# One product set for keys and queries of four heads, placed by ten DMAs, in a fused vision-transformer kernel

## The chip, the cores and the metric

The program runs on one core of a Trainium2 chip. The time is the device time of one execution in microseconds (us). Engines: PE (TensorE, matrix products), DVE (VectorE), ACT (ScalarE), POOL (GpSimd), SP (SyncE, which here only issues DMAs). Each engine runs its own instructions in program order and waits on semaphores that the others raise. "Hop" below is the time between the end of one operation and the start of the one on another engine that it releases.

## What is computed

For each of 128 images (3 x 224 x 224) the kernel computes a patch embedding (196 tokens of 192 numbers, a layer norm before and after), a causal attention with 12 heads of 16 dimensions and a relative term, and a routed block (sigmoid score per token; the 29 tokens of the lowest scores get attention over all tokens, the others a gated mixture; then an MLP 192-768-192 with gelu). Cut to what the change touches:

```python
h = tok(x)                                   # patches, LN, @W + b, LN
qkv = LN(h) @ w_attn + b_attn                # q, k, v; 12 heads of 16
q = q * 16 ** -0.5
scores = q @ k.T + q @ rel.T                 # so the keys are k + rel
probs = softmax(where(causal, scores, -inf))
h = h + (probs @ v) @ w_proj + b_proj
h = h + routed_block_and_mlp(LN(h))
```

## The kernel before

All weights stay in SBUF. Products that need near-float32 accuracy are made in a reduced format (F32R) from parts: a number is a high part plus a low part, and a product takes `PAIRS`, five matmuls over the two chunks of the 192 input columns. T is 196 tokens, HT 98, NG 3 groups of four heads.

**Four images are in work at once.** A pass of the loop (`step(k, m, n, l, ...)`, L313) does the last stage (`tail`: the MLP's `up`, gelu, `down`, `output`) for image k, the middle (`back`: the routed block) for k + 1, the causal attention (`front`) for k + 2 and the embedding (`head`) for k + 3. Each engine has the calls of a pass written out by hand in one fixed order; that order is the schedule. The steady loop makes 124 passes; passes before and after fill and drain it. PE's list also has 36 matmuls for keys and queries in each pass.

**Keys and queries before.** At the start of a pass PE's `keys` and `queries` (both through `group_cols`, L698 to L712) make for each of the three groups a [128, 196] product: five matmuls with `wk` or `wq` (L705) and one for bias and relative term (L711, L708). Of the 128 output rows, a head has 32: its 16 dimensions twice ("doubled columns"), the first 16 for the high part, the second 16 for the low part. ACT copies (L1589, L1584), DVE makes the low part (L1230, L1224). The keys go to `kparts`, and SP's `place_keys` (L428) puts them with four DMAs of 32 partitions into `kz`, where head s has its own columns and the other heads' rows are zero; queries stay in `qparts`. A score unit (`causal("S0")` to `"S8"`, L740 and L743) multiplies `qparts` by four heads of `kz`.

**Around it on PE**, in the order of a pass: `routed_cols` (transposes of `z`, L679), `score` and `keys2` (L695, `nTs`), `mlp_cols` (L679), `values` (L687, `wv`), `values2`, `mixing_rows` (L687), S0 to S2, `gather`, S3, `weighted_sum`, `qsel` (L857), S4, `embed(0)` (L754), S5 to S7, `scores2` (L865 to L867, needs DVE's `q_blocks`), S8, `square_sums`, transposes A0 to B2 (L778) between `embed(1)`, `up(0)`, `transposes2`, `up(1)` and `context2`, then `attention` (L929, L936: the sum over values, called y), `attn_out` (L907), `up(2)`, `projection` (L948), `scatter`, `attention_cols` (L679, `a_row`), `down` (L982).

**Around it on DVE and POOL.** DVE: `routed_cols_lo` (L1209, L1211), `q_blocks` (L1356, L1359), `max2` (L1365, L1368), `embedding` (L1274 with its statistics L1187 and L1190), `h1_stats` (L1187, `bn_a`), `attention_input` (L1195, `a_row`). POOL: nine `normalised` units (L539), `rstd` (L512, L514), the softmax division of the routed block (L584, "pn2" below), the two operations that make `h1` (L596, L598), `gelu_low` (L530).

Of the kernel before, what the change touches and what calls it, by code (L numbers as in the profile page):

```python
# [38 lines left out]
T = GR * GR  # L39
# [29 lines left out]
    x_in=len(XROWS) * 16, out_done=16, kz_in=4 * 16,  # L69

    tok_mm=1, sqs_mm=1, zT_mm=1, score_mm=1, mrow_mm=1, usum_mm=1, kk_mm=1, vv_mm=1, aT_mm=1, q_mm=1, k_mm=1, v_mm=1,
# [4 lines left out]
    tok_var=1, tok_y=1, y_stat=1, y_norm=1, h1_stat=1, a_sb=1, aTs_sb=1, klo_sb=1,  # L76
    qparts_sb=1, rowmax=9, rden_sb=9, pT_dve=len(PT) - len(PT_ACT), h2_sb=1,
# [3 lines left out]
    sq_sb=1, aT_sb=1, qhi_sb=1, khi_sb=1, v_sb=1, probs=9, pT_act=len(PT_ACT), yhi_sb=2,  # L81
# [14 lines left out]
def build(nc, ins, out):  # L96
    W = dict(ins)
    with ExitStack() as ctx:
# [32 lines left out]
        widths = dict(wq=NG * 128, wk=NG * 128, wv=D, fwk=D, fwv=D, fwm=D, wr=HT, w1=F)  # L131
        split = {name: sb(name + "_split", [128, 4, width], F32R)
                 for name, width in widths.items()}
        bk = sb("bk", [128, NG])
# [3 lines left out]
        relk = sb("relk", [128, NG, T], F32R)  # L138
        add_parts = sb("add_parts", [128, 128], F32R)
        onesr = sb("onesr", [128, T], F32R)  # L140
        bqparts = sb("bqparts", [128, NG * 128], F32R)
# [42 lines left out]
        qk_parts = sb("qk_parts", [128, 2, NG, T], F32R)  # L184
        qhi, qparts = (qk_parts[:, i] for i in range(2))

        table_out = sb("table_out", [1, 1])
        kz = sb("kz", [128, 2, 4, NG, T], F32R)
# [10 lines left out]
        yhi, yparts = qhi, qparts  # L199
# [55 lines left out]
        kparts = gparts[:, :, 0:NG]  # L255
# [7 lines left out]
        relb = flat[:, 2 * F:2 * F + NG * T].rearrange("p (g t) -> p g t", g=NG)  # L263
# [6 lines left out]
        bqrow = p0[:].rearrange("p h t -> p (h t)")[:, 0:NG * 128]  # L270
# [3 lines left out]
        for i, name in enumerate(("wq", "wk")):  # L274
            size = 2 * widths[name]
            raw[name] = flat[:, i * size:(i + 1) * size].rearrange("p (c w) -> p c w", c=2)
# [109 lines left out]
        for s in range(4):  # L386
            for r in (0, DH):
                at = 32 * s + r
                load(bk[at:at + DH], ba[1, s])
                load(wp[at:at + DH], wpr[s])  # L390
# [1391 lines left out]
```

## Time and profile before

| | |
|---|---|
| median of 3 runs | 5028.85 us (5027.4 to 5029.55) |
| the profiled execution, its own time | 5031.06 us |
| its span, first to last instruction | 5029.3 us |
| PE busy | 4843.7 us, 96% |
| DVE, ACT, POOL busy | 79%, 70%, 64% |
| DMA engines, mean busy | 43.3% |
| granted TensorE clock, mean | 0.988 |

A PE that counts as busy is one with a matmul in flight; since matmuls overlap, the length of a stretch is read from the start of one group to the start of the next, not from the groups' own lengths. The loop repeats exactly: the attention product of one pass starts at 2500.43 us, that of the next at 2538.41, 37.98 us later. A row of the timeline gives start, length, engine, line, operation, operands, count, and in brackets the idle time ahead of it with what ended it.

### The profile page before, as it was taken

The numbers are of one execution on the slowest core, as the hardware profiler recorded it, in microseconds if no ns is written. First come the engines' busy times: TensorE is split into PE (matmuls) and PEld (weight loads), VectorE is DVE, ScalarE is ACT, GpSimd is POOL, SyncE is SP. The second block draws the span as 40 slices with busy tenths as digits, with TensorE's granted clock in tenths as the row PEclk, the third lists the DMA queues.
The fourth block names the chain that finished last, engine by engine and source line by source line (L and its number), as shares of the span: only waits on it lengthen the run. The fifth ranks groups of instructions, "written<-read, shape, count | busy, mean of one in ns | idle before, by whom it ended". The sixth has DMA issues, their size and how long they took to land. (4 is left out here: it accounts for less than half of the span.)

```text
span 5029.3 us, 146877 instructions
## 1 busy us (share of the span) xinstructions
PE 4843.7 (96%) x46680; PEld 4523.8 (90%) x46680; DVE 3993.2 (79%) x12888; ACT 3540.8 (70%) x12158; POOL 3230.6 (64%) x4399
## 2 busy tenths in 40 slices
PE   3999999999999999999999999999999999999998
PEld 2899999999999999999999999999999999999997
DVE  3788888888888888888888888888888888888885
ACT  0677777776777777777777677777777777777775
POOL 2566666666666666666666666666666666666664
PEclk6999999999999999999999999999999999999999
DMA  5444444444444445444444444444444444444440
GB/s 68 56 65 62 55 64 61 59 62 61 61 59 64 61 55 67 62 55 65 61 59 62 61 61 59 64 61 56 67 62 55 65 61 59 62 61 61 59 64 16
DMA packets 338231, 302.00 MB, mean 60 GB/s; under 512 B 46796, under 2 KB 305177, under 8 KB 338201
## 3 DMA queue, kind: packets, MB, share of 16 engines
q1 hardware_dynamic: 325950, 298.98, 43.3%
q10 hardware_dynamic: 12251, 2.65, 0.4%
q8 instruction: 15, 0.25, 0.0%
q14 instruction: 15, 0.12, 0.0%
HBM read 205.18 MB, written 19.27 MB: 45 GB/s over the span
## 5 line engine op out<-in xcount | busy, mean ns | idle before, releaser
L1615 ACT ACTIVATE p<-banks,negmax 98x98 f32<-98x98 f32 (+1 forms) x3072 | 1138.9, 379 | 184.8 <-DVE negmax L1237 121.3
L539 POOL TENSOR_TENSOR p<-p,rden 98x392 f32<-98x392 f32 x1152 | 953.6, 842 | 384.0 <-DVE rden L1253 379.5
L1237 DVE TENSOR_REDUCE negmax<-banks 98x2 f32<-98x392 f32 (+1 forms) x1152 | 626.2, 553 | 51.4 <-PE banks L743 51.2
L743 PE MATMUL banks<-kz,qk_parts 128*98 128x392 f32 x2304 | 632.8, 385 | 0.0
L778 PE MATMUL banks<-ident,p 98*98 98x98 f32 x4608 | 550.7, 251 | 69.9 <-ACTq L1619 64.4
L1615 ACT ACTIVATION_READ_ACCUMULATOR p<-banks,negmax 98x1 f32 x3072 | 610.3, 199 | 0.0
L754 PE MATMUL banks<-tokw,x_sb 128*98 128x193 f32 x3072 | 572.7, 336 | 15.5 <-POOLq L551 15.5
L530 POOL TENSOR_TENSOR gparts<-gT,gparts 128x392 fp32r<-128x392 f32 x384 | 398.3, 1050 | 270.8 <-DVE gparts L1433 270.8
L754 PEld LDWEIGHTS banks<-tokw,x_sb 128*98 128x98 f32 x3072 | 541.7, 252 | 18.0 <-issue 15.5
L778 PEld LDWEIGHTS banks<-ident,p 98*98 98x98 f32 x4608 | 415.8, 129 | 140.0 <-ACTq L1619 90.8
L695 PE MATMUL banks<-z3Ts,w_split 128*128 128x196 f32 x3840 | 534.7, 286 | 4.8 <-DVE z3Ts L1211 3.9
L695 PEld LDWEIGHTS banks<-z3Ts,w_split 128*128 128x128 f32 x3840 | 477.9, 194 | 9.1 <-DVE z3Ts L1211 4.9
L982 PE MATMUL banks<-w,gparts 128*98 128x192 f32 x4608 | 441.2, 254 | 2.6 <-issue 2.6
L554 POOL TENSOR_TENSOR gstore<-gstore 128x588 f32<-128x588 f32 x128 | 155.2, 1213 | 447.0 <-ACT gstore L1600 447.0
L1690 ACT ACTIVATE gT<-banks,bf 128x196 f32<-128x196 f32 x768 | 285.5, 426 | 206.6 <-PE banks L695 206.6
L1680 ACT ACTIVATE f<-h,shift,rstdf 98x192 f32<-98x192 f32 x256 | 126.5, 541 | 426.3 <-DVE shift L1449 426.3
L982 PEld LDWEIGHTS banks<-w,gparts 128*98 128x98 f32 x4608 | 422.5, 164 | 2.9 <-issue 2.9
L514 POOL TENSOR_TENSOR rstd<-ve,nhalf 98x2 f32<-98x2 f32 x512 | 360.5, 704 | 72.7
L1623 ACT COPY pT<-banks 98x392 f32<-98x392 f32 x768 | 358.7, 480 | 68.1 <-PE banks L778 50.2
L743 PEld LDWEIGHTS banks<-kz,qk_parts 128*98 128x98 f32 x2304 | 322.1, 166 | 40.3
L740 PE MATMUL banks<-tri,identh 98*98 98x196 bf16 (+1 forms) x1152 | 323.3, 281 | 5.4 <-DMA kz<-gparts 3.8
L1593 ACT ACT_TABLE_LOAD x252 | 323.3, 1283 | 4.5
(273 smaller groups left out, 12470.1 us busy)
## 6 DMA issues: line engine op xcount, KB each, us to landing
x_sb<-in_x SPq DMA_DIRECT2D x384, 196.0 KB, 5.0
kz<-gparts SPq DMA_DIRECT2D x512, 147.0 KB, 2.9
x_sb<-in_x SPq DMA_DIRECT2D x256, 190.8 KB, 8.8
x_sb<-in_x SPq DMA_DIRECT2D x256, 185.5 KB, 10.9
x_sb<-in_x SPq DMA_DIRECT2D x128, 189.0 KB, 7.3
out<-out_row SPq DMA_DIRECT2D x128, 147.0 KB
pT<-in_L_ffn_W ACTq DMA_DIRECT2D x1, 576.0 KB
gstore<-in_L_ffn_W SPq DMA_DIRECT2D x1, 384.0 KB
```

What stands on the lines that cost most here:

```text
L514: gp.tensor_tensor(r, ve, nhalf[:], ALU.pow).then_inc(sem[name], 1)
L530: gp.tensor_tensor(gparts[:, 1, at], gT[:, j % 2], gparts[:, 0, at].bitcast(F32), ALU.subtract).then_inc(sem["gparts_sb"], 1)
L539: gp.tensor_tensor(heads, heads, rden[:, g, t, s0:s0 + sn].unsqueeze(2).broadcast_to([HT, sn, w]), ALU.mult).then_inc(sem["pnorm_sb"], 1)
L695: last = mm(o, w[:, wpart, lo:hi], src[:, p], start=i == 0, stop=i == len(PAIRS) - 1)
L740: mm(masked, identh[:], tri[:].unsqueeze(1).broadcast_to([HT, len(slots), HT]), start=True, stop=False, skip_group_check=True)
L743: last = mm(o, qparts[:, g, HT * t:HT * t + HT], kz[:, part, slots[0]:slots[-1] + 1, g, 0:w], start=False, stop=part == 1, skip_group_chec ...
L754: last = mm(bank[b][0:HT, t * (D + 1):(t + 1) * (D + 1)], xf[:, a:a + (HT - 1) * PS + 1:PS], tokw[:, q], start=t == 0 and q == 0, stop=q = ...
L778: last = pe.transpose(bank[b][0:HT, HT * i:HT * i + HT], src, ident[0:HT, 0:HT])
L982: last = mm(bank[7][0:HT, t * D:(t + 1) * D], gparts[:, part, f, HT * t:HT * t + HT], w2[:, wpart, f], start=f == 0 and t == 0 and i == 0, ...
L1237: ve.tensor_reduce(negmax[:, g, t, slots[0]:slots[-1] + 1], bank[RING[f"S{k}"]][0:HT, 0:w * len(slots)].rearrange("p (s w) -> p s w", w=w) ...
L1615: sc.activation((p1 if t else p0)[0:HT, 4 * g + s], bank[b][0:HT, w * i:w * i + w], ACT.Exp, bias=negmax[:, g, t, s:s + 1], accum_out=den[ ...
L1623: sc.copy(pt_dst(name[0], int(name[1:])), bank[RING[name]][0:HT, 0:4 * HT]).then_inc(sem["pT_act"], 1)
```

## The change

Keys and queries of four heads (a group) come out of one product set: the weight `wkq` has for each group 64 columns of keys and 64 of queries, without doubling, so that 18 matmuls a pass take the place of 36. Bias and relative term come in one matmul per group (`add_w`, `rel_ones`). ACT makes the high part of all 128 rows (`kq[:, 0]`), DVE the low part (`kq[:, 1]`). High and low parts of the scores' operands then have to be on different partitions, and that is now done by DMAs: eight of 16 partitions put the keys of a head twice into `kz`, two of 64 partitions put the queries into `qparts` (high part to partitions 0 to 63, low to 64 to 127). They start when the low part is there (`kqlo_sb`), and S0 waits for them (`kz_in`, `q_in`).

The product set is moved from the start of the pass that uses it to the end of the pass before, between `scatter` and `down`; `attention_cols` moves ahead of `up(2)` and writes bank 2 (was 1); the attention product y goes to banks 0 and 1 (was 2 and 3). `yhi` and `yparts` are tiles of their own. SP issues the placement after the next image's prefetch. The order of many other calls changes on all engines: `embed(0)` ahead of `values2`, `embed(1)` after S4, `qsel` after it, `up(0)` and `up(1)` together before S8, `transposes2` and `context2` earlier, `attn_out` before B2.

```diff
@@ SP @@
-                sp.wait_ge(sem["klo_sb"], after("klo_sb", n))
+                sp.wait_ge(sem["kqlo_sb"], after("kqlo_sb", n))
                 for s in range(4):
-                    at = slice(32 * s, 32 * s + 32)
-                    sp.dma_start(kz[at, :, s].bitcast(F32),
-                                 kparts[at].bitcast(F32)).then_inc(sem["kz_in"], 16)
+                    for r in range(2):
+                        at = 64 * r + DH * s
+                        sp.dma_start(kz[at:at + DH, s].bitcast(F32),
+                                     kq[DH * s:DH * s + DH].bitcast(F32)).then_inc(
+                                         sem["kz_in"], 16)
+                for part in range(2):
+                    sp.dma_start(qparts[64 * part:64 * part + 64].bitcast(F32),
+                                 kq[64:128, part].bitcast(F32)).then_inc(sem["q_in"], 16)
...
             with sp.Fori(0, B - 4) as j:
-                place_keys(j + 2)
                 prefetch(j + 3, j + 4)
+                place_keys(j + 3)
                 store(j)
@@ PE @@
-                def queries():
-                    if back:
-                        pe.wait_ge(sem["h2_sb"], all_before("h2_sb", n))
-                    pe.wait_ge(sem["aTs_sb"], after("aTs_sb", n))
-                    group_cols(0, split["wq"], "q_mm")
+                    pe.wait_ge(sem["aTs_sb"], after("aTs_sb", l))
+                    for g in range(NG):
+                        o, at = grouped(2)[:, g], slice(128 * g, 128 * g + 128)
+                        for i, (p, wpart) in enumerate(PAIRS):
+                            mm(o, split["wkq"][:, wpart, at], aT[:, p], start=i == 0, stop=False)
+                        last = mm(o, add_w[:, at], rel_ones[:], start=False, stop=True)
+                    last.then_inc(sem["kq_mm"], 1)
...
                         if k == 0:
-                            pe.wait_ge(sem["qparts_sb"], after("qparts_sb", n))
+                            if back:
+                                pe.wait_ge(sem["h2_sb"], all_before("h2_sb", n))
+                            pe.wait_ge(sem["q_in"], after("q_in", n))
                             pe.wait_ge(sem["kz_in"], after("kz_in", n))
...
-                    out_of = [bank[2 + g // 2][:, (g % 2) * T:(g % 2) * T + T] for g in range(NG)]
+                    out_of = [bank[g // 2][:, (g % 2) * T:(g % 2) * T + T] for g in range(NG)]
@@ DVE @@
                 def keys():
 
-                    ve.wait_ge(sem["khi_sb"], after("khi_sb", n))
-                    ve.tensor_tensor(kparts[:, 1], grouped(2), kparts[:, 0].bitcast(F32),
-                                     ALU.subtract).then_inc(sem["klo_sb"], 1)
+                    ve.wait_ge(sem["kqhi_sb"], after("kqhi_sb", l))
+                    ve.tensor_tensor(kq[:, 1], grouped(2), kq[:, 0].bitcast(F32),
+                                     ALU.subtract).then_inc(sem["kqlo_sb"], 1)
@@ the loads of the weights, once @@
-                for j, name in enumerate(("wq", "wk")):
-                    for r in (0, DH):
-                        load(raw[name][p:p + size, chunk].rearrange(
-                                 "p (h e) -> p h e", e=32)[:, :, r:r + DH],
-                             wa[lo:hi, j * D:(j + 1) * D].rearrange("p (h e) -> p h e", e=DH))
+                for j, at in enumerate((D, 0)):
+                    load(halves(raw["wkq"][p:p + size, chunk])[:, j],
+                         wa[lo:hi, at:at + D].rearrange("p (g w) -> p g w", g=NG))
```

**PE, from the attention product into the next pass.** Before (the two branch rows are the turn of the loop; the group of five and one stands three times for each product set):

```order
L948 MATMUL banks<-wps,qk_parts 98x192 x12
L915 MATMUL banks<-ao,selT 98x192 x4
L679 MATMUL banks<-ident,a_row 128x98 x2
L679 MATMUL banks<-ident,a_row 64x98 x2
L982 MATMUL banks<-w,gparts 98x192 x36
L313 UNCONDITIONAL_BRANCH
L313 ISA
L705 MATMUL banks<-aT,wk_split 128x196 x5
L711 MATMUL banks<-relk,add_parts 128x196
```

After:

```order
L699 MATMUL banks<-z3Ts,w_split 128x196 x10
L943 MATMUL banks<-wps,yparts 98x192 x12
L910 MATMUL banks<-ao,selT 98x192 x4
L718 MATMUL banks<-aT,wkq_split 128x196 x5
L719 MATMUL banks<-rel_ones,add_w 128x196
...
L977 MATMUL banks<-w,gparts 98x192 x36
L313 UNCONDITIONAL_BRANCH
L313 ISA
L683 MATMUL banks<-ident,z 128x98 x2
```

The product set now stands ahead of `down` (L982, now L977), and a pass begins with the transposes of `z`; the queries' set, which stood between those transposes and `score`, is gone.

**DVE, from `q_blocks` to the statistics of the embedding.** Before (`max2` is the two reductions to 128 partitions; rows of `z3Ts`, `pT`, `mean`, `var` and others follow it, and L1274 of `embedding` comes thirteen rows on):

```order
L1365 TENSOR_REDUCE negmax<-banks 128x2
L1368 TENSOR_REDUCE negmax<-banks 128x1
L1208 REGISTER_ALU
L1209 TENSOR_TENSOR z3Ts<-banks,z3Ts 128x196
L1211 TENSOR_TENSOR z3Ts<-banks,z3Ts 64x196
L1253 RECIPROCAL rden<-den 98x4
L1245 COPY pT<-banks 98x392
```

After:

```order
L1345 TENSOR_TENSOR qb<-qs,slot_of 128x256
L1348 TENSOR_TENSOR qb<-qs,slot_of 64x128
L1224 REGISTER_ALU
L1226 TENSOR_REDUCE negmax<-banks 98x2
L1224 REGISTER_ALU
L1226 TENSOR_REDUCE negmax<-banks 98x4
L1242 RECIPROCAL rden<-den 98x2
L1354 TENSOR_REDUCE negmax<-banks 128x2
L1357 TENSOR_REDUCE negmax<-banks 128x1
L1242 RECIPROCAL rden<-den 98x2
L1263 SCALAR_TENSOR_TENSOR y_row<-banks,rstd,tok_bias 98x192 x2
L1182 BN_STATS bn_y<-y_row 98x6 x2
```

`embedding` stands right behind `max2`, so it cannot start before `scores2` has been made.

**POOL, from the embedding's second `rstd` to `h1`.** Before:

```order
L584 TENSOR_TENSOR probs_<-probs_,rden 128x588
L537 REGISTER_ALU
L539 TENSOR_TENSOR p<-p,rden 98x392
L512 TENSOR_TENSOR ve<-mv_y,epsc 98x2
```

After:

```order
L516 TENSOR_TENSOR ve<-mv_y,epsc 98x2
L518 TENSOR_TENSOR rstd<-ve,nhalf 98x2
L586 TENSOR_TENSOR probs_<-probs_,rden 128x588
L541 REGISTER_ALU
L543 TENSOR_TENSOR p<-p,rden 98x392
```

Pn2 stood ahead of that `rstd` and stands behind it now, with three `normalised` units after it (two of which stood ahead of it before) and then the two operations for `h1`.

## Rows read from the trace of the kernel before

**Rows 1.** Timeline of PE: start us, length us, line, operands, count, [idle ahead].

```profile
2505.58 3.43 PE L982 MATMUL banks<-w,gparts 128*98 128x192 f32 x36
2508.84 0.73 PE L705 MATMUL banks<-aT,wk_split 128*128 128x196 f32 x5
...
2510.86 0.50 PE L679 MATMUL banks<-ident,z 98*128 98x98 f32 x4
2511.14 0.78 PE L705 MATMUL banks<-aT,wq_split 128*128 128x196 f32 x5
...
2515.10 1.11 PE L687 MATMUL banks<-wv_split,aT 128*98 128x192 f32 x10
2517.85 0.33 PE L740 MATMUL banks<-tri,identh 98*98 98x392 bf16 x1
...
2525.04 0.25 PE L740 MATMUL banks<-tri,identh 98*98 98x196 bf16 x1
...
2526.45 0.49 PE L865 MATMUL banks<-kk,qb 128*128 128x196 f32 x2
...
2527.45 0.25 PE L740 MATMUL banks<-tri,identh 98*98 98x196 bf16 x1
...
2528.54 2.26 PE L754 MATMUL banks<-tokw,x_sb 128*98 128x193 f32 x12
2530.50 1.40 PE L695 MATMUL banks<-z3Ts,w_split 128*128 128x196 f32 x10
...
2533.06 0.88 PE L778 MATMUL banks<-ident,p 98*98 98x98 f32 x8 [0.48 <-ACTq L1619]
...
2540.62 1.39 PE L695 MATMUL banks<-z3Ts,w_split 128*128 128x196 f32 x10
```

**Rows 2.** Timeline of ACT, same pass.

```profile
2511.60 0.33 ACT L1572 CAST nTs<-banks 128x196 fp32r<-128x196 f32 x1
...
2522.64 0.46 ACT L1561 ACTIVATE qs<-banks,fbqs 128x32 f32<-128x32 f32 x2 [0.68 <-PE banks L857]
```

**Rows 3.** Timeline of DVE, same pass.

```profile
2511.74 0.77 DVE L1230 TENSOR_TENSOR gparts<-banks,gparts 128x588 fp32r<-128x588 f32 x1 [0.42 <-ACT gparts L1589]
...
2512.79 0.36 DVE L1211 TENSOR_TENSOR nTs<-banks,nTs 64x196 fp32r<-64x196 f32 x1
...
2519.07 0.65 DVE L1321 TENSOR_SCALAR ez<-ez 98x2 f32<-98x2 f32 x1
...
2523.47 0.28 DVE L1359 TENSOR_TENSOR qb<-qs,slot_of 64x128 f32<-64x128 f32 x1
...
2527.79 0.55 DVE L1365 TENSOR_REDUCE negmax<-banks 128x2 f32<-128x392 f32 x1
...
2532.64 0.74 DVE L1274 SCALAR_TENSOR_TENSOR y_row<-banks,rstd,tok_bias 98x192 f32<-98x192 f32 x2 [0.54 <-POOL rstd L514]
...
2539.60 0.60 DVE L1187 BATCH_NORM_STATS2 bn_a<-h 98x6 f32<-98x192 f32 x2
...
2541.97 0.65 DVE L1195 TENSOR_SCALAR a_row<-h,mv_a,rstd 98x192 f32<-98x192 f32 x2
```

**Rows 4.** Timeline of POOL, same pass.

```profile
2518.98 0.72 POOL L558 TENSOR_TENSOR sqsum<-gstore 128x196 f32<-128x196 f32 x1
...
2532.56 1.17 POOL L584 TENSOR_TENSOR probs_<-probs_,rden 128x588 f32<-128x588 f32 x1
...
2535.49 0.84 POOL L539 TENSOR_TENSOR p<-p,rden 98x392 f32<-98x392 f32 x1
...
2537.96 1.01 POOL L598 TENSOR_TENSOR h<-y_row,ln2b 98x384 f32<-98x384 f32 x1
```

**Rows 5.** Timeline of SP's DMA queue, same pass.

```profile
2512.54 2.52 SPq L431 DMA_DIRECT2D kz<-gparts  x4
```

**Rows 6.** The page, section 6: DMA issues, KB each, median us from issue to landing.

```profile
kz<-gparts SPq DMA_DIRECT2D x512, 147.0 KB, 2.9
```

**Rows 7.** Timeline of DVE at the start of the program.

```profile
55.51 0.46 DVE L1091 COPY pT<-bv 128x294 f32<-128x294 f32 x1 [30.33 <-DMA pT<-in_L_ffn_W]
```

More of the change, by code:

```diff
@@ L565, in step @@
                     normalised(1)
-                if back:
-                    gp.drain()
-                    gp.tensor_tensor(h2b[:], h2[:], both(bf2), ALU.add).then_inc(sem["h2b_sb"], 1)
+                if head:
+                    gp.wait_ge(sem["tok_var"], after("tok_var", l))
+                    rstd(var1[:], ve1[:], rstd1[:], "tok_rstd")
                 if front:
@@ L576, in step @@
                     normalised(5)
[L577 to L578 removed]
                 if head:
[L580 to L581 removed]
+                    gp.wait_ge(sem["y_stat"], after("y_stat", l))
+                    rstd(mv_y[:, :, 1], ve2[:], rstd2[:], "y_rstd")
                 if back:
@@ L587, in step @@
                 if front:
+                    normalised(6)
+                if front:
                     normalised(7)
-                if head:
-                    gp.wait_ge(sem["y_stat"], after("y_stat", l))
-                    rstd(mv_y[:, :, 1], ve2[:], rstd2[:], "y_rstd")
                 if front:
@@ L603, in step @@
                     rstd(mv_a[:, :, 1], ve3[:], rstd3[:], "h1_rstd")
+                if tail:
+                    gelu_low(0)
+                if back:
+                    gp.drain()
+                    gp.tensor_tensor(h2b[:], h2[:], both(bf2), ALU.add).then_inc(sem["h2b_sb"], 1)
                 if tail:
@@ L990, in attention_cols @@
                     pe.wait_ge(sem["a_sb"], after("a_sb", l))
-                    rows_to_cols(1, a_row, "aT_mm")
-                if front:
-                    keys()
+                    if front:
+                        pe.wait_ge(sem["pT_act"], after("pT_act", n, evacuation("B1")[1]))
+                    rows_to_cols(2, a_row, "aT_mm")
                 if back:
@@ L997, in step @@
                 if front:
-                    queries()
+                    values()
+                if tail:
+                    mlp_cols()
                 if back:
@@ L1001, in step @@
                     keys2()
-                if tail:
-                    mlp_cols()
-                if front:
-                    values()
+                if head:
+                    embed(0,0,QX)
                 if back:
@@ L1022, in step @@
                 if head:
-                    embed(0,0,QX)
+                    embed(1,0,3)
+                    embed(1,3,QX)
+                if back:
+                    qsel()
                 if front:
@@ L1059, in step @@
                     attention()
-                if back:
-                    attn_out()
+                if head:
+                    attention_cols()
                 if tail:
@@ L1068, in step @@
                 if head:
-                    attention_cols()
+                    keys()
                 if tail:
@@ L1698, in step @@
                 if front:
+                    values()
                     load_table(ACT.Exp)
-                    queries()
                 if back:
+                    exp_scores()
                     keys2()
+                if tail:
+                    mlp_cols_hi()
                 if head:
```

249 lines of the change are left out of this document (107 added, 142 removed).

## The prediction

> **What bounds the kernel now.** I read the busy shares first, then the period of the loop, then one pass of the timeline on each engine. PE is busy 96% of the span, DVE, POOL and ACT less (the table under the profile's heading), so PE's list of matmuls sets the time. The loop repeats at 37.98 us, and 37.98 x 124 is 4710 of 5029 us; what the change does to one pass counts about 125 times. PE's timeline of a pass marks a single wait of size, 0.48 us ahead of the transposes at 2533.06, for ACT's softmax; everything else starts where the group before it lets go [rows 1]. I put another 0.5 us into gaps too short for the timeline to mark, by a count of columns against the distances between groups: an estimate. So waits hold PE for about 1.0 us of a pass, and removed matmuls are worth their full length only as long as nothing that PE waits for becomes the later one. That is the question of this change: PE gets shorter, and the chains through ACT, DVE, POOL and now SP get no shorter.
>
> **Removed matmuls.** The keys' set of 18 holds PE from 2508.84 to 2510.86, 2.02 us, 0.112 us a matmul [rows 1]. Half of 36 go: -2.02 us a pass. The remaining 18 have the same shapes.
>
> **Placement and S0.** Before, `keys` ends at 2510.86 and SP's first placement goes out at 2512.54 [rows 5]: 1.68 us for ACT's copy and DVE's low part, which itself takes 0.77 [rows 3]. Four issues take 2.52 us, 0.63 each, and one lands 2.9 us after its issue [rows 5, 6]. After, ten go out: nine spacings of 0.63 are 5.67, and the last lands 2.9 later, 8.57. From the end of the product set to S0's data: 1.68 + 8.57 = 10.25 us. PE's work in that time: the stretch from `down` to S0, 2505.58 to 2517.85, is 12.27 us and holds both product sets, 2 x 2.02; `embed(0)` comes into it, as long as its twin `embed(1)`, 2528.54 to 2530.50, 1.96 [rows 1]. So 12.27 - 4.04 + 1.96 = 10.19, and with a wait of 0.3 for `score` (below) 10.5. The placement is hidden by 0.25 us, hence at nothing, with all of that work as its cover; each 0.1 us that it is later costs 12.5 us in all. Eight of the ten carry half the bytes (16 partitions), and if spacing follows bytes the sum falls to 1.68 + 8 x 0.32 + 0.63 + 2.9 = 7.8: slack 2.7. If instead an issue waits for engines that work on few partitions, it grows; the lower end is no cost, the upper one is the second rival. I take no cost, since the nearest row counts issues and I gave it no credit for size. SP's prefetch now stands ahead of the placement and its store behind; the prefetch waits for buffers that are free long before, which I cost at nothing.
>
> The Trainium skill speaks against the shape of these DMAs. Its page "SBUF — State Buffer", section "Door 1: The DMA port swizzle", has it that bandwidth follows how many of 16 ports the partitions reach, with 104 GB/s on 16 partitions and 189 on 32. By that price alone a DMA of 16 partitions would take 0.7 us of transfer, about what one of 32 with twice the bytes takes, eight and two in a row some 7.3 us, and the last would land at 11 us after the product set instead of 10.25. The rows of before hold only DMAs of 32 partitions, so no row here decides it.
>
> **Three legs whose cover shrinks.** On each, PE waits for other engines' answer to its own product.
>
> (a) *From `scores2` to `attention_cols`.* `embedding` now stands behind `max2` on DVE, pn2 and three `normalised` units stand between the embedding's second `rstd` and h1 on POOL. The chain: from the end of `scores2` (the group behind it starts at 2527.45 [rows 1]) to DVE's start at 2527.79 is 0.34, then 0.55 and about 0.3 for the second, smaller reduction, and a reciprocal, 0.1: 1.3 [rows 3]. From `embedding`'s L1274 at 2532.64 to POOL's unit behind `rstd` at 2535.49: 2.85. Pn2: 1.17. Three units at 0.84, packed a little closer: 2.4. The two operations of h1, 1.01 each with a drain between: 2.15 [rows 3, 4]. From `bn_a` at 2539.60 to the end of `a_row` at 2542.62: 3.02, of which 0.4 goes, because `gelu_low` no longer stands ahead of that `rstd`; a hop, 0.1. Sum: 1.3 + 2.85 + 1.17 + 2.4 + 2.15 + 2.62 + 0.1 = 12.6 us. PE's work from the end of `scores2` to `attention_cols`: 2527.45 to 2540.62 is 13.17, less `embed(1)` 1.96, the wait 0.48, square sums 0.3 and the short gaps 0.3, plus S7, 0.45: 10.6 [rows 1]. So PE waits 2.0 us in this leg whatever it does; the first of it, about 0.9, at `transposes2`, which needs pn2 (1.3 + 2.85 + 1.17 = 5.3 us behind `scores2`, where PE has 4.4 us to do), then at `attn_out` and `attention_cols`. With hops counted twice here and there I take 1.9; the ends are 1.4 and 2.3.
>
> (b) *From `qsel` to `scores2`.* ACT's `qs` starts at 2522.64, DVE's `qb` ends at 2523.47 + 0.28: 1.11 us, with two hops 1.35 [rows 2, 3]. Before, PE had S4, `embed(0)` and S5 to S7 to do there. Now it has S5 and S6: three such units take 2525.04 to 2526.45, two 0.95 [rows 1]. PE waits 0.4 (0.2 to 0.6).
>
> (c) *From the transposes of `z` to `score`.* Before, the queries' set, 2 us, covered ACT's and DVE's copies into `nTs`: ACT starts at 2511.60, DVE ends at 2512.79 + 0.36, 1.55 us [rows 2, 3], of which up to 0.4 is `kparts`' low part (0.77) in the way, now gone. The cover is now `values`, about 1.0, and `mlp_cols`, the same four transposes as 2510.86 to 2511.14, 0.28 [rows 1]. With a hop: a wait of 0.3 (0 to 0.45).
>
> New waits: 1.9 + 0.4 + 0.3 = 2.6 us. The old ones, 1.0, go, since their causes lie inside the longer ones: a PE that has waited finds the softmax behind it done. The pass: -2.02 + 2.6 - 1.0 = **-0.4 us**, 37.98 to 37.6; over 125 passes -50 us. With the ends of the terms: -1.2 to +0.2 us a pass.
>
> **One-time parts.** At the start DVE waits 30.33 us for the last weight load [rows 7]; fourteen loads fewer, and runs of 64 bytes made into runs of 256, let that end earlier. I take -10 (-18 to -4). Filling the pipeline costs a placement of ten with nothing to hide it, +4 to +5. On ACT and DVE the new parts are as many copies of 588 columns less one pair; neither engine is the bound. The banks of y and its own tiles take a reuse wait away and cost nothing: DVE has `a_row` (0.65 [rows 3]) done as the last of leg (a), not behind y.
>
> **Sum.** -50 - 10 + 5 = -55. The profiled execution took 5031.06, 2.2 above the median of 5028.85; against the median: 4974, say **4975 us**.
>
> **Rivals.** *The full gain.* If the chains are shorter than I add them up (units run beside one another closer, or the new order leaves no queue), PE's saving shows: -2.02 x 125 = -253, with the one-time parts 4770; with half of the new waits (-2.02 + 1.3 - 1.0) x 125 = -215, 4810; with three quarters 4890. For it: PE at 96%. Against it: the order of DVE and POOL, which puts leg (a) in a row. Chance 0.15.
>
> *The placement ends last, slower.* S0 waits for `kz_in` and `q_in`. The point is 0.25 us of lateness behind 10.25. If a DMA of 16 partitions holds its queue for as long as one of 32 and lands as late as the second half of them (each issue 0.72 instead of 0.63, landing 3.3), S0's data come at 1.68 + 6.5 + 3.3 = 11.5, 1.0 us late; a part of it takes the place of the wait in leg (c) and of leg (a)'s, which starts over behind S6 and does not shrink, so 0.5 to 0.8 us a pass stay: 4975 + 62 to 100 = 5037 to 5075. At 0.2 us it is 5000. For it: DVE's and PE's work is all ahead of it in one line. Against it: half the bytes. Chance 0.17, 0.12 of it slower.
>
> *`q_blocks` is held by POOL.* DVE's `ez`, two numbers a partition, takes 0.65 us and ends at 2519.72; POOL's operation beside it ends at 2519.70 [rows 3, 4]. DVE operations on SBUF do wait here for POOL's. `q_blocks` reads two SBUF tiles and now stands, by my sum, 0.2 us clear of a `normalised` unit of 0.84. If it falls behind it, leg (b) and everything behind `scores2` are later by up to 0.84, about 0.7: +88, **5060 us**. Chance 0.08. The Trainium skill, page "SBUF — State Buffer", section "SBUF: two separate sides", calls this pair of ports an exclusive lock, held for the whole instruction, also for a DVE operation with two SBUF inputs against a POOL one that reads SBUF; the `ez` rows agree, and by that rule such an operation waits as computed.
>
> *It does nothing that shows*: the set is halved and another order of the same waits gives the period back, 5020 to 5038. Chance 0.05.
>
> **How the numbers follow.** Forecast 0.55 (its own range 4950 to 5000), full or half gain 0.15, placement 0.17, held `q_blocks` 0.08, nothing 0.05. A measurement of this kernel tells 0.2%, 10 us, from no change. Faster by more: 0.55 + 0.15 + 0.02 = 0.72; within it 0.03 + 0.05 = 0.08; slower 0.12 + 0.08 = 0.20. The range leaves out the fuller gains (0.08) and the later placements and a held `q_blocks` (0.12): 4905 to 5050.
>
> **What the profile after would show.** Right: a period of 37.6 us; 18 matmuls in 2.0 us behind `scatter`; marked PE waits at `transposes2` (0.9, for POOL's pn2), `attn_out` (0.5), `scores2` (0.4, for DVE's `qb`) and `score` (0.3); S0 without a wait; ten placements at 0.63 or closer, landing 2.9; the idle time at the start shorter by some 10. Wrong: S0 idle ahead of it for a DMA (the placement); `qb`'s L1359 longer than 0.28, or late (the lock); marked waits under 2 us a pass (the full gain), or over 3.5, which would say that a chain I added up has another link.

## The result and the profile after

The changed kernel takes 4967.28 us, the median of 4 runs (4967.15 to 4967.44), against 5029.01 (4 runs, 5027.4 to 5029.55): a ratio of 0.9878, 95% interval 0.9861 to 0.9895. That is 61.7 us less, where 54 were forecast. Its profiled execution has a span of 4965.4 us, 63.9 less than the one of before.

The page of the changed kernel, section 1, columns as in the table of before, and section 6:

```profile
PE 4645.9 (94%) x44376; PEld 4282.1 (86%) x44376; DVE 3884.0 (78%) x12759; ACT 3468.4 (70%) x12030; POOL 3263.1 (66%) x4399
...
kz<-kq SPq DMA_DIRECT2D x1024, 73.5 KB, 2.6
...
qparts<-kq SPq DMA_DIRECT2D x256, 147.0 KB, 2.7
```

PE is busy for 197.8 us less and the span is 63.9 us shorter, so PE's idle time grew by 134 us. The waits of PE that the profile marks, in the whole execution (us in total, times, longest):

```profile
PE banks L869 <- POOL probs_ L586: 93.2, 127, 2.7
PE banks L902 <- DVE ctxT L1378: 37.7, 127, 1.4
PE banks L683 <- DVE a_row L1190: 37.5, 125, 10.5
...
PE banks L699 <- DVE y_row L1263: 23.6, 125, 0.2
PE banks L699 <- DVE nTs L1206: 19.2, 118, 0.7
```

The kernel before had one such row of size that comes back in every pass:

```profile
PE banks L778 <- ACTq L1619: 64.4, 130, 1.5
```

One pass of PE's timeline, changed kernel, what answers to [rows 1]:

```profile
2506.76 0.87 PE L902 MATMUL banks<-fwo,ctxT 128*66 128x192 f32 x4 [0.28 <-DVE ctxT L1378]
...
2509.82 0.55 PE L683 MATMUL banks<-ident,a_row 98*128 98x98 f32 x4 [0.21 <-DVE a_row L1190]
...
2512.77 0.73 PE L718 MATMUL banks<-aT,wkq_split 128*128 128x196 f32 x5
...
2514.78 3.38 PE L977 MATMUL banks<-w,gparts 128*98 128x192 f32 x36
...
2519.24 0.50 PE L683 MATMUL banks<-ident,z 98*128 98x98 f32 x4
2519.89 0.70 PE L699 MATMUL banks<-nTs,wr_split 128*98 128x196 f32 x5 [0.16 <-DVE nTs L1206]
...
2525.34 0.33 PE L733 MATMUL banks<-tri,identh 98*98 98x392 bf16 x1
...
2533.03 0.33 PE L733 MATMUL banks<-tri,identh 98*98 98x392 bf16 x1
...
2533.81 0.60 PE L860 MATMUL banks<-kk,qb 128*128 128x196 f32 x2
...
2536.80 1.33 PE L699 MATMUL banks<-z3Ts,w_split 128*128 128x196 f32 x10 [0.18 <-DVE y_row L1263]
2537.98 0.25 PE L733 MATMUL banks<-tri,identh 98*98 98x196 bf16 x1
...
2538.42 0.84 PE L771 MATMUL banks<-ident,p 98*98 98x98 f32 x8
2539.98 0.86 PE L869 MATMUL banks<-ident,probs_ 128*98 128x128 f32 x6 [0.72 <-POOL probs_ L586]
...
2542.81 1.22 PE L771 MATMUL banks<-ident,p 98*98 98x98 f32 x12
2544.32 0.87 PE L902 MATMUL banks<-fwo,ctxT 128*66 128x192 f32 x4 [0.29 <-DVE ctxT L1378]
```

`attn_out` (L902) starts at 2506.76 and at 2544.32. A single pass differs from the next by some hundredths of a microsecond, so the period is better read over many: between the fourth and the 126th `attn_out` are 122 passes, from 291.51 to 4872.24 us here (37.55 each) and from 297.85 to 4934.69 before (38.01). 0.46 x 124 = 57 us is the loop's part of the 63.9. The periods of the experiments below are read over one or two passes. The product set lies between 2512.77 and 2514.78, 2.01 us for 18 matmuls. S0 (2525.34) has no wait marked. Between S6 (2533.03) and `scores2` (2533.81) are 0.78 us; a unit of four heads has 0.54 elsewhere in the pass (S3, 2527.74 to 2528.28), so 0.25 is a wait for `qb` that isn't marked.

**What a mark leaves out.** A mark counts idle time from the end of the last matmul as the profile draws it, and that end lies behind the point where the next one could have started. The eight transposes at 2538.42 have a row of 0.84 us; in `v_diag2` below, where nothing is waited for behind them, the next group starts 0.69 after the first of them (2526.45 to 2527.14). Here it starts 1.56 after (2538.42 to 2539.98): a delay of 0.87 where the mark says 0.72. A delay below some 0.15 (0.84 less 0.69) can stay without a mark. So delays are read below from start to start, against the same group where nothing holds it. The same reading of the kernel before:

```profile
2531.74 0.84 PE L778 MATMUL banks<-ident,p 98*98 98x98 f32 x8
...
2535.95 1.04 PE L778 MATMUL banks<-ident,p 98*98 98x98 f32 x8
2536.92 1.09 PE L884 MATMUL banks<-scratch,vv 98*64 98x128 f32 x12
```

From 2531.74 to 2533.06 [rows 1] are 1.32 us for eight transposes, a delay of 0.6 where the mark says 0.48, and from 2535.95 to 2536.92 are 0.97, a delay of 0.25 without a mark. S3 takes 0.73 (2520.26 to 2520.99) where a unit of four heads has 0.54, another 0.2.

POOL and SP, same pass of the changed kernel:

```profile
2533.20 0.41 POOL L516 TENSOR_TENSOR ve<-var,epsc 98x2 f32<-98x2 f32 x1 [1.99 <-DVE var L1256]
...
2534.42 3.24 POOL L543 TENSOR_TENSOR p<-p,rden 98x392 f32<-98x392 f32 x4
...
2538.76 1.17 POOL L586 TENSOR_TENSOR probs_<-probs_,rden 128x588 f32<-128x588 f32 x1
2539.88 2.47 POOL L543 TENSOR_TENSOR p<-p,rden 98x392 f32<-98x392 f32 x3
...
2543.45 1.00 POOL L599 TENSOR_TENSOR h<-y_row,ln2b 98x384 f32<-98x384 f32 x1
```

```profile
2516.46 5.00 SPq L429 DMA_DIRECT2D kz<-kq  x8
2521.50 1.24 SPq L433 DMA_DIRECT2D qparts<-kq  x2
```

From 2533.20 to 2544.45 POOL works almost without a gap: leg (a) runs through its queue. SP issues ten placements in 6.28 us, 0.62 to 0.63 apart, those of 16 partitions as those of 64.

At the start of the program, DVE's wait for the last weights, and SP's first loads of `w_attn`, in the changed kernel and (second fence) in the kernel before:

```profile
46.50 0.46 DVE L1085 COPY pT<-bv 128x294 f32<-128x294 f32 x1 [20.48 <-DMA pT<-in_L_ffn_W]
...
14.34 3.34 SPq L411 DMA_DIRECT2D p<-in_L_attn_w_attn  x2
```

```profile
14.19 10.45 SPq L414 DMA_DIRECT2D p<-in_L_attn_w_attn  x3
```

Such a row merges issues. The three of before, each read in a window of its own (the second starts at 14.77, the third at 21.76): 0.54 and 6.95 us for two loads of 128 rows in runs of 64 bytes, then 2.88 for the values' weights, which have runs of 768. The two of after: 0.58 for one in runs of 256, 2.72 for the values' weights.

The wait is 9.9 us shorter than in [rows 7]; at the first `a_row` the changed kernel is 10.6 us ahead (98.48 against 109.07 us).

### The profile page after: what moved, and what is told of

Its sections match the earlier page's. It is cut to its first block and busy times, and to the rows that moved or that the text cites. A ratio compares the mean times of both kernels' runs of the same rounds, so it can differ in the third digit from the quotient of the medians.

```text
span 4965.4 us, 143019 instructions
## 1 busy us (share of the span) xinstructions
PE 4645.9 (94%) x44376; PEld 4282.1 (86%) x44376; DVE 3884.0 (78%) x12759; ACT 3468.4 (70%) x12030; POOL 3263.1 (66%) x4399
## 5 line engine op out<-in xcount | busy, mean ns | idle before, releaser
L736 PE MATMUL banks<-kz,qparts 128*98 128x392 f32 x2304 | 650.7, 386 | 0.0
L1226 DVE TENSOR_REDUCE negmax<-banks 98x2 f32<-98x392 f32 (+1 forms) x1152 | 614.9, 550 | 40.6 <-PE banks L736 40.5
L699 PE MATMUL banks<-z3Ts,w_split 128*128 128x196 f32 x3840 | 508.3, 280 | 25.8 <-DVE y_row L1263 23.6
L771 PE MATMUL banks<-ident,p 98*98 98x98 f32 x4608 | 481.6, 250 | 3.6 <-ACTq L1600 3.6
L977 PE MATMUL banks<-w,gparts 128*98 128x192 f32 x4608 | 434.3, 252 | 0.5 <-POOL gparts L534 0.4
L977 PEld LDWEIGHTS banks<-w,gparts 128*98 128x98 f32 x4608 | 422.9, 163 | 0.8 <-POOL gparts L534 0.8
L1604 ACT COPY pT<-banks 98x392 f32<-98x392 f32 x768 | 343.7, 478 | 40.7 <-PE banks L771 28.4
L736 PEld LDWEIGHTS banks<-kz,qparts 128*98 128x98 f32 x2304 | 321.8, 166 | 28.6
L1570 ACT CAST kq<-banks 128x588 fp32r<-128x588 f32 x128 | 83.2, 650 | 350.7 <-PE banks L719 350.7
## 6 DMA issues: line engine op xcount, KB each, us to landing
kz<-kq SPq DMA_DIRECT2D x1024, 73.5 KB, 2.6
```

Source lines behind the costliest of these rows:

```text
L699: last = mm(o, w[:, wpart, lo:hi], src[:, p], start=i == 0, stop=i == len(PAIRS) - 1)
L736: last = mm(o, qparts[:, g, HT * t:HT * t + HT], kz[:, slots[0]:slots[-1] + 1, part, g, 0:w], start=False, stop=part == 1, skip_group_chec ...
L771: last = pe.transpose(bank[b][0:HT, HT * i:HT * i + HT], src, ident[0:HT, 0:HT])
L977: last = mm(bank[7][0:HT, t * D:(t + 1) * D], gparts[:, part, f, HT * t:HT * t + HT], w2[:, wpart, f], start=f == 0 and t == 0 and i == 0, ...
L1226: ve.tensor_reduce(negmax[:, g, t, slots[0]:slots[-1] + 1], bank[RING[f"S{k}"]][0:HT, 0:w * len(slots)].rearrange("p (s w) -> p s w", w=w) ...
L1604: sc.copy(pt_dst(name[0], int(name[1:])), bank[RING[name]][0:HT, 0:4 * HT]).then_inc(sem["pT_act"], 1)
```

## The experiments

**The matmuls alone.** The kernel before with three matmuls for each group instead of six; nothing else is touched.

```diff
-                    for i, (p, wpart) in enumerate(PAIRS):
+                    for i, (p, wpart) in enumerate(PAIRS[:2]):
```

> The kernel before, its order unchanged, with three matmuls instead of six in each of the six groups for keys and queries: 18 matmuls a pass are gone (the other products of the parts are left out, so keys and queries are coarse), and nothing is placed, moved or reordered. If PE's list alone sets the time: 2.02 us a pass less, 5029 - 253 = 4776 us. If the legs through the other engines take it back: the queries' set (now 1.07 us) covers less of the copies into nTs, so that PE waits some 1.0 to 1.4 us at score, and only 0.6 to 0.9 us a pass are left: 4917 to 4955 us.

Measured: 4969.22 us, ratio 0.9872 (0.9856 to 0.9889), some 60 us less than before. The period is 37.53 us (two passes of `attn_out`, 2469.98 to 2545.03), the same as the changed kernel's. PE's waits name the place (the old wait for ACT's softmax stays, 64.2 us in all):

```profile
PE banks L695 <- DVE nTs L1211: 179.5, 127, 2.1
```

1.41 us a pass are marked at `score`. From start to start, 1.69 us lie between the queries' last matmul and `score`, in the mean of the loop's passes, where the kernel before has 0.18: 1.51 of delay have come. -2.02 + 1.51 = -0.51, and the period fell by 0.48 (38.01 to 37.53): this account closes. The legs theory holds, PE's list alone does not, though even the legs theory was 14 us too hopeful. It is also the best measure of the new order: with 18 matmuls less, the old order got as much while it waited in one new place as the new one gets while it waits in six. (It couldn't have them without the new placement, since there the parts of 64 columns lie elsewhere.)

**The order with the old matmuls.** The changed kernel, product set made twice in its place.

```diff
-                        for i, (p, wpart) in enumerate(PAIRS):
-                            mm(o, split["wkq"][:, wpart, at], aT[:, p], start=i == 0, stop=False)
-                        last = mm(o, add_w[:, at], rel_ones[:], start=False, stop=True)
+                        for again_ in range(2):
+                            for i, (p, wpart) in enumerate(PAIRS):
+                                mm(o, split["wkq"][:, wpart, at], aT[:, p], start=i == 0, stop=False)
+                            last = mm(o, add_w[:, at], rel_ones[:], start=False, stop=True)
```

> The changed kernel with its product set of 18 matmuls made twice, in the place where it stands: the new order, placement and banks with as many matmuls as before. If the removed matmuls are worth their full 2.02 us at that place and the rest of the gain was lost by the new order's waits: 2.0 us a pass more, 4969 + 254 = 5223 us, some 190 us above the kernel before. If the new order were no worse than the old one with the same matmuls: 5029 us.

Measured: 5222.14 us, ratio 1.0387 (1.0369 to 1.0404). The period is 39.59 us (2474.69 to 2553.86 in two passes), 2.05 more than the changed kernel's. At this place, between `scatter` and `down`, outside every leg, a matmul costs and saves its full length, and all waits of the changed kernel stay as they were. So the change of -0.46 is -2.05 for the matmuls and +1.6 for waits that order and shorter cover bring, less the old ones that went.

**Ten matmuls outside and inside leg (a).** Both double a product of ten matmuls in the changed kernel.

```diff
@@ values2 @@
-                    cols_to_rows(5, nTs, split["fwv"], "vv_mm")
+                    for part in range(2):
+                        for t in range(2):
+                            for i, (p, wpart) in enumerate(PAIRS):
+                                last = mm(bank[5][0:HT, t * D:(t + 1) * D],
...
@@ up @@
-                    for f in (2 * j, 2 * j + 1):
+                    for f in (2, 3, 2, 3) if j == 1 else (2 * j, 2 * j + 1):
```

> The changed kernel with values2 made twice: ten more matmuls of 192 columns, 0.9 to 1.0 us, between embed(0) and S0, outside the leg from scores2 to attention_cols. Both theories expect the full price, 0.9 to 1.0 us a pass: 5080 to 5093 us. A result much below that would say that S0 was waiting for something that the trace does not mark.

> The changed kernel with up(1) made twice: ten more matmuls of 196 columns, 1.2 us, between scores2 and transposes2. If PE's list sets the time: 1.2 us a pass, 5117 us. If POOL and DVE set the time of the leg from scores2 to attention_cols, the waits at transposes2 (0.72), attn_out (0.28) and attention_cols (0.21) take it up, all but what S8's softmax and its copies come later: 0.3 to 0.8 us a pass, 5005 to 5067 us, with the wait for pn2 at transposes2 gone.

Measured: `values2` twice 5079.67 us, ratio 1.0094 (1.0077 to 1.0111), a period of 38.46 (2481.66 to 2558.57 in two), +0.92: the full price. `up(1)` twice 5042.66 us, ratio 1.0021 (1.0012 to 1.0031), a period of 38.14 (2465.97 to 2542.24), +0.60. In the timeline of PE of the second kernel:

```profile
2533.88 2.45 PE L699 MATMUL banks<-z3Ts,w_split 128*128 128x196 f32 x20 [0.19 <-DVE y_row L1263]
2536.16 0.25 PE L733 MATMUL banks<-tri,identh 98*98 98x196 bf16 x1
...
2537.29 0.82 PE L869 MATMUL banks<-ident,probs_ 128*98 128x128 f32 x6
...
2539.72 1.09 PE L879 MATMUL banks<-scratch,vv 98*64 98x128 f32 x12 [0.44 <-ACT scratch L1643]
```

The wait of 0.72 for pn2 and that of 0.21 for `a_row` are gone, a new one of 0.44 for ACT's copies has come. `up(1)` now lasts 2.28 us (to S8 at 2536.16) where it lasted 1.18 (2536.80 to 2537.98): 1.10 - 0.72 - 0.21 + 0.44 = 0.61, measured 0.60. (Marks leave something out on both sides of this sum; from start to start, in the mean of the loop's passes, it is 1.12 - 0.92 - 0.27 + 0.67 = 0.60.) The wait of 0.29 at `attn_out` stays. Work in leg (a) is half free, outside it is not.

**Two more placements.** The changed kernel with two further DMAs of 16 partitions ahead of the ten, into a spare tile, counted by `kz_in`.

```diff
+                for s in range(2):
+                    sp.dma_start(spare[16 * s:16 * s + 16].bitcast(F32),
+                                 kq[16 * s:16 * s + 16].bitcast(F32)).then_inc(sem["kz_in"], 16)
```

> The changed kernel with two more DMAs of 16 partitions (75 KB each, into a spare tile) ahead of the ten. If an issue costs 0.62 us whatever its size, the last data land 1.25 us later; S0 had 0.5 us to spare, so PE waits 0.75 us there each pass: 5060 us. If spacing follows bytes and only the larger ones take 0.62, or if the legs behind S0 take the lateness up, nothing or up to 0.2 us a pass: 4967 to 4992 us.

Measured: 5118.12 us, ratio 1.0169 (1.0152 to 1.0186), a period of 38.72 (2466.95 to 2544.39 in two), +1.18. PE and SP:

```profile
2525.34 0.36 PE L738 MATMUL banks<-tri,identh 98*98 98x392 bf16 x1 [0.95 <-DMA qparts<-kq]
```

```profile
2515.37 1.19 SPq L428 DMA_DIRECT2D spare<-kq  x2
2516.60 5.03 SPq L434 DMA_DIRECT2D kz<-kq  x8
2521.67 1.24 SPq L438 DMA_DIRECT2D qparts<-kq  x2
```

Two issues take 1.23 us, and 1.18 of it is paid. My 0.5 us of room, taken from the median landing of 2.7, was wrong: here S0 starts 3.05 us behind the last issue (2522.29 to 2525.34), and with that the changed kernel has 0.05 to 0.2 us. The waits of leg (a) stayed as they were (pn2 95.2 us in all, 93.2 before), so nothing behind S0 takes lateness up. The second theory, spacing by bytes, falls: 73.5 KB take the 0.62 us of 147 KB.

**POOL's pn2 taken away.** DVE multiplies the identity by the reciprocal sums, the transposes of the routed probabilities take these matrices, and POOL's division is gone.

```diff
@@ DVE, inverse2 @@
+                    ve.tensor_tensor(diag2[:], ident[:].unsqueeze(1).broadcast_to([128, NG, 128]),
+                                     rden2[:].unsqueeze(2).broadcast_to([128, NG, 128]),
+                                     ALU.mult).then_inc(sem["pn2_sb"], 1)
@@ PE, transposes2 @@
-                            last = pe.transpose(bank[4 + t][0:HT, 128 * g:128 * g + 128],
-                                                probs2[:, g, HT * t:HT * t + HT], ident[:])
+                            last = mm(bank[4 + t][0:HT, 128 * g:128 * g + 128],
+                                      probs2[:, g, HT * t:HT * t + HT], diag2[:, g],
+                                      start=True, stop=True)
```

> The changed kernel without POOL's pn2: DVE multiplies the identity by the reciprocal sums (128 x 384, about 0.5 us, right behind inverse2) and the transposes of the routed probabilities multiply by that instead of by the identity, which divides them. If POOL's queue sets leg (a): the wait of 0.72 at transposes2 and the one of 0.21 at attention_cols go, but a wait of 0.3 to 0.5 for ACT's copies ahead of context2 comes: -0.3 us a pass, 4930 us (4905 to 4945). If something else sets the leg: 4967 or more.

Measured: 4947.56 us, ratio 0.984 (0.9824 to 0.9857); period 37.38 (2495.06 to 2569.81 in two). Half of the gain expected. PE's timeline:

```profile
2526.45 0.84 PE L767 MATMUL banks<-ident,p 98*98 98x98 f32 x8
2527.14 1.55 PE L865 MATMUL banks<-diag,probs_ 128*98 128x128 f32 x12
2528.53 1.18 PE L767 MATMUL banks<-ident,p 98*98 98x98 f32 x12
2529.91 1.09 PE L876 MATMUL banks<-scratch,vv 98*64 98x128 f32 x12 [0.21 <-ACT scratch L1644]
```

The waits of 0.72 and 0.21 are gone as expected, but six products stand as 12 matmuls and last 1.39 us, where six transposes lasted 0.70: in the trace a product of two f32 operands is two matmuls, a transpose one. I had priced them alike.

**All divisions of two-head units as well.** Six of the nine `normalised` units write diagonal matrices of 98 x 196 instead of dividing 98 x 392, and A's second halves and B multiply by them; the second kernel puts calls in another order on top.

```diff
-                        last = pe.transpose(bank[b][0:HT, HT * i:HT * i + HT], src, ident[0:HT, 0:HT])
+                            last = mm(o, p1[0:HT, h, HT * u:HT * u + HT], diag1[:, h], start=True, stop=True)
```

> As v_diag2, and the six normalised units of two heads (98 x 392 on POOL) make diagonal matrices too (98 x 196), which the transposes A and B take in place of the identity: POOL is some 2 us a pass less busy. If POOL still set leg (a) after v_diag2 this brings more, 4890 to 4915 us; if the leg by then runs through ACT and DVE (context2, attn_out), as the waits that I expect of v_diag2 say, nothing: 4925 to 4935 us.

> v_both with another order of calls: on DVE maxima(4), mixing_rows, embedding and inverse2 shifted by one or two places, embedding behind maxima(7); on PE gather behind S2, S4 ahead of square_sums, attn_out behind B2, up(1) behind S8; on POOL h1_with_bias between the first units and h2b ahead of the two operations of h1. If with POOL unburdened the order is what holds PE at scores2, context2 and attn_out: 36.85 us a pass, 0.7 less than the changed kernel, 4880 us (4870 to 4905). If not, as v_both.

Measured: 5161.87 us, ratio 1.0265 (1.0248 to 1.0282), and with the other order 5177.49, ratio 1.0297 (1.0279 to 1.0314). Neither theory allowed for it. The second matmul of each f32 product is why: a pair of one transpose and one product now reads

```profile
2516.17 0.25 PE L773 MATMUL banks<-ident,p 98*98 98x98 f32 x1
2516.26 0.34 PE L770 MATMUL banks<-diag,p 98*98 98x98 f32 x2
2516.43 0.25 PE L773 MATMUL banks<-ident,p 98*98 98x98 f32 x1
```

0.09 us for the transpose, 0.17 for the product; 24 products a pass cost 2 us of PE. POOL's operation fell from 844 to 522 ns, and no wait of leg (a) but the small one for `y_row` is left on PE's list (`ctxT` and `a_row` no longer appear in the loop). With these waits gone the period is nearer to PE's list alone, at 39.07 us a pass (2484.08 to 2523.15); two delays outside the leg grew as well, at S0 for the placement (`mixing_rows` to S0 1.22 us in the mean, 0.90 in the changed kernel) and at `score` by 0.1. It says nothing against POOL having set leg (a); it says what the cure cost.

**One matmul instead of two.** As v_diag2, with `probs2` and `diag2` in the reduced format F32R, whose products are one matmul each (the projection's weights, which were staged in `probs2` at the start, are staged in `p1`); and then the same with some calls a place or two earlier or later.

```diff
-        diag2 = sb("diag2", [128, NG, 128])
+        diag2 = sb("diag2", [128, NG, 128], F32R)
-        probs2 = sb("probs2_", [128, NG, T])
+        probs2 = sb("probs2_", [128, NG, T], F32R)
```

> As v_diag2 (4948 us), but the routed probabilities and the diagonal matrices are in the reduced format, so that each of the six products takes one pass and not two: 0.6 to 0.7 us for the six, where v_diag2 took 1.31 and the transposes of the changed kernel 0.70. If PE's list sets the time there now: 0.6 us a pass less than v_diag2, 4872 us. If leg (a) still runs through ACT and DVE (the copies of the transposes, context2, ctxT), half or more of it is waited away ahead of context2: 0.1 to 0.3 us a pass, 4910 to 4935 us.

> v_diag2r with some calls shifted by a place or two: S7 behind up(0) and up(1) behind S8 on PE; maxima(3), mix, maxima(4) and inverse_sums(3) on DVE nearer to what they wait for; softmax(8) behind A1's copy and gelu(0) behind the copies on ACT. If ACT's and DVE's queues hold context2 and scores2 there: 0.1 to 0.2 us a pass less than v_diag2r, by 12 to 25 us. If these waits are the legs' own lengths: the same as v_diag2r within 5 us.

Measured: 4942.08 us, ratio 0.982 (0.9804 to 0.9837), the fastest of all that were run; with the other order 4949.55, ratio 0.9831 (0.9814 to 0.9847). The period of the first is 37.36 us (2492.49 to 2567.20 in two):

```profile
2524.55 0.74 PE L865 MATMUL banks<-diag,probs_ 128*98 128x128 f32 x6
2525.13 0.51 PE L767 MATMUL banks<-ident,p 98*98 98x98 f32 x4
2526.01 0.88 PE L767 MATMUL banks<-ident,p 98*98 98x98 f32 x8 [0.37 <-ACTq L1601]
2527.32 0.87 PE L876 MATMUL banks<-scratch,vv 98*64 98x128 f32 x10 [0.44 <-ACT scratch L1644]
```

PE is 0.8 us a pass shorter here than in v_diag2 (0.58 for 1.39) and the period is 0.02 shorter: all of it is waited, 0.37 for ACT's softmax of S8, 0.44 for ACT's copies. Leg (a) now runs through ACT. The second order trades: waits at `scores2` (40.1 us in all, for `qb`) and at the routed transposes (35.9) appear in place of a shorter one, and nothing is won.

**Banks undone.** The changed kernel with y in banks 2 and 3 and the transposes of `a_row` in bank 1, as before.

```diff
-                    out_of = [bank[g // 2][:, (g % 2) * T:(g % 2) * T + T] for g in range(NG)]
+                    out_of = [bank[2 + g // 2][:, (g % 2) * T:(g % 2) * T + T] for g in range(NG)]
-                    rows_to_cols(2, a_row, "aT_mm")
+                    rows_to_cols(1, a_row, "aT_mm")
```

> The changed kernel with y back in banks 2 and 3 and attention_cols back in bank 1: that part undone. The product set, which writes banks 2 and 3, stands behind projection, and that waits for y's copies anyway: 4967 to 4972 us, no difference. If the product set had to wait for DVE's copies of y longer than projection does: +0.2 us a pass or more, 4992 us and up.

Measured: 4963.08 us (4957.91 to 4966.22), ratio 0.9862 (0.9846 to 0.9879), which overlaps the changed kernel's own interval. Its period is 37.50 (2502.32 to 2577.32 in two), 0.04 less, if anything better. The banks of y brought nothing. (`attention_cols` also waits there for all of ACT's copies and no longer for some of them.)

**Short runs at the start.** The changed kernel with six more loads in runs of 64 bytes.

```diff
+                for r in (0, DH):
+                    load(flat[p:p + size, 768 + 384 * chunk:768 + 384 * chunk + 384].rearrange(
+                             "p (h e) -> p h e", e=32)[:, :, r:r + DH],
+                         wa[lo:hi, 0:D].rearrange("p (h e) -> p h e", e=DH))
```

> The changed kernel with six more weight loads at the start, in runs of 64 bytes (the queries' weights twice into unused columns), as half of the kernel before's had been; the loop is the same. In the kernel before three such loads held SP's queue for 10.45 us, 3.5 each for those of 128 rows. If the runs' number is what the start waits for: DVE's wait for the last weights goes from 20.5 to some 25 us, and the time to 4971 to 4976 us. If other loads set it: 20 to 21 us and no difference.

Measured: 4971.03 us (4970.26 to 4971.52), ratio 0.9875 (0.9859 to 0.9892), 3.8 us above the changed kernel, less than the intervals tell apart; but the trace shows the place:

```profile
50.58 0.46 DVE L1089 COPY pT<-bv 128x294 f32<-128x294 f32 x1 [24.19 <-DMA pT<-in_L_ffn_W]
...
14.44 9.93 SPq L415 DMA_DIRECT2D p<-in_L_attn_w_attn  x3
```

DVE's wait is 3.7 us longer, and the first three issues of `w_attn` hold SP's queue for 9.93 us. The expectation says three short-run loads of before did that, at 3.5 us each; that was misread. Of the three here only one has runs of 64 bytes: 0.61 us for the one in runs of 256, 2.92 for the short one, 6.33 for the values' weights behind it. The six loads give back 4.1 of the 9 us by which the last weights had come earlier (55.51, 50.58, 46.50). They are more loads as well as short runs, so the run doesn't tell the two apart.

## Why the prediction was right, step by step

The delays are read from start to start, in us a pass (against the same group where nothing holds it, as said below the profile after):

| term | foretold | the rows show |
|---|---|---|
| removed matmuls | -2.02 | -2.0 (set 2.01 long, 2.05 when doubled) |
| leg (a): `transposes2` | 0.9 | 0.87 |
| leg (a): `attn_out` | 0.5 | 0.40 (2542.81 to 2544.32 is 1.51 for twelve transposes, 1.11 at 2540.68) |
| leg (a): `attention_cols` | 0.5 | 0.29 (the last group of `attention` takes 0.57 and took 0.28) |
| leg (a): `up(1)`, for `y_row` | none | 0.2 (2535.36 to 2536.80 is 1.44 for `up(0)`; 2530.50 to 2531.74, 1.24, before) |
| leg (b): `scores2` | 0.4 | 0.25 ahead of it and 0.1 within |
| leg (c): `score` | 0.3 | 0.37 (2519.24 to 2519.89 is 0.65 for four transposes, 0.28 in [rows 1]) |
| all new waits | 2.6 | 2.5 |
| old waits gone | -1.0 | -1.1 (0.6 and 0.25 ahead of transposes, 0.2 in S3, under 0.1 at `score`) |
| the pass | -0.4 | -0.46 |

- **Bound.** That PE's list sets the time, and that the chains through the others would take most of the gain, is what the runs show: 2.0 us removed, 0.46 kept.
- **Leg (a).** The leg is 12.45 us long, from the end of `scores2` to `attention_cols`, against 12.6: DVE starts `embedding` 1.0 behind `scores2` instead of 1.3, and the links through POOL came out as added up (2.83, 1.12, 2.43, 2.14 us against 2.85, 1.17, 2.4, 2.15). POOL's queue is the mechanism, as given, for the waits at `transposes2` and `attention_cols`, which both go when pn2 leaves POOL. The other two stay in that run. `up(1)` waits for `embedding`, which stands behind `max2` on DVE; the forecast had that order but no wait from it. `attn_out` keeps its 0.29 also when `up(1)` is doubled: that is a leg of its own, from `context2` through DVE back to PE, with too little cover.
- **Legs (b) and (c).** Both inside their ranges.
- **Old waits.** The 0.5 in gaps too short to be marked was right: the rows of before have 0.12 beyond the mark, 0.25, 0.2 and under 0.1. By the marks alone it looks otherwise (1.39 + 0.25 + 0.16 = 1.8 of new waits, and 0.48 of old), and one would take two terms for wrong by 0.8 each; it is the marks that are short.
- **What is left.** -2.0 + 2.5 - 1.1 is -0.6 and the pass is -0.46. The remaining 0.1 to 0.2 us are in steps of at most 0.13 at groups that have other neighbours now (`values2` takes 1.02 and took 0.89, `attn_out` 0.70 and 0.57); what makes them isn't shown.
- **Placement.** 1.68 us from the end of the set (2514.78) to the first issue (2516.46), as foretold; ten issues at 0.62 to 0.63, as foretold; hidden by 0.05 to 0.2 us, foretold 0.25. The rival stood closer than its chance of 0.17 says: two more DMAs of 73.5 KB would have made of the gain of 62 us a loss of 89. The page's price (the Trainium skill, "SBUF — State Buffer", section "Door 1: The DMA port swizzle") would have had the last data at 11 us and S0 0.5 late; S0 isn't late. Here the issues' spacing of 0.62 decided, the same over 16 partitions as over 64, and not the ports.
- **q_blocks and the lock.** Not held: 0.43 and 0.28 us as before (L1345, L1348). But no `normalised` unit ran beside it, since the next one starts at 2534.42, 0.66 us behind it; so the rival didn't get its chance, and what such a unit would have cost isn't shown. The only operation beside it was POOL's small `ve` at 2533.20, which took 0.41 us where it took 0.20 in the kernel before. `embedding_normalised` took 1.20 us for two operations beside POOL's units, as before (1.18), against 0.67 for two of the same shape elsewhere (`a_row`).
- **Start.** -10.6 against -10, with both of the reasons given, fourteen loads fewer (102 for 116) and longer runs. How much each brought isn't shown. SP's first issues of `w_attn` are through after 3.34 us and not after 10.45.
- **Fill and drain.** 57 + 10.6 - 63.9 leaves 3.7 of loss, foretold 5: at the first `attn_out` the lead is down from 10.6 to 6.0 us (175.56 against 181.53), and S0 of the first image waits 5.9 us for its queries, where it had waited 3.8 for its keys.

So the prediction was right by its mechanism and by the size of its terms; the one wait that it didn't see (0.2, at `up(1)`) made up for the excess in its other terms of leg (a).

## What to carry to other kernels

Before work is taken off the bounding engine, list the legs that leave it and come back, and compare each with the work it has left in between; here 2.0 us were removed, 2.5 came in six places and 1.1 of old waits went. A doubled group of matmuls inside and outside a leg measures this in two runs: 0.92 of 0.9 to 1.0 us outside, 0.60 of 1.10 inside. When a sum comes out right, compare its terms with the rows too, and read delays from start to start: the marks of idle time showed 1.39 of the 1.76 us of leg (a), and of the four delays that went in the kernel before they showed one.

## What the runs showed of the hardware

- An issue of a placement from SP costs 0.62 to 0.63 us whether it moves 73.5 KB over 16 partitions or 147 KB over 32 or 64; eight small ones took 5.00 us, two large ones 1.24. Halving a DMA and doubling their number doubles the time.
- A product that divides (or scales) as it transposes costs twice a transpose in f32 (0.17 against 0.09 us for 98 columns; 1.39 against 0.70 for six of 128) and no more than one in the reduced format (0.58 for six).
- A load holds SP's queue for a time that its own size doesn't tell. The first `w_attn` load in runs of 64 bytes took 0.54 us to issue and the same one behind it 6.95; the values' weights took 2.88 in the kernel before, 2.72 in the changed one and 6.33 behind a short-run load in `e_runs`; eight later short-run loads of 64 rows took 0.62 to 0.77 us each. What holds the long ones isn't shown.
- DVE's operation on two numbers a partition (`ez`) took 0.65 us beside an operation of POOL [rows 3, 4] and 0.16 in the changed kernel, where POOL has nothing to do at that moment:

```profile
2523.79 0.16 DVE L1310 TENSOR_SCALAR ez<-ez 98x2 f32<-98x2 f32 x1
```
